# A gated linear-attention and recurrence kernel: one tile's normalisation shared with ScalarE, a subtraction in halves, and two orders on TensorE changed

## The reference, cut to what matters

```python
Q = elu(x @ Wq.T + bq) + 1;  K = elu(x @ Wk.T + bk) + 1;  V = x @ Wv.T + bv
KV = einsum('bnd,bne->bde', K, V)
Z  = einsum('bnd,bd->bn', Q, K.sum(axis=1) + 1e-06)
x1 = layernorm(x + (Q @ KV / Z) @ Wo.T + bo)
# recurrence over the first axis of x1
ft = sigmoid(xt @ wf.T + c @ uf.T + bf);  it = sigmoid(xt @ wi.T + c @ ui.T + bi)
gt = tanh(xt @ wc.T + c @ uc.T + bc);     c = ft * c + it * gt
h  = tanh(x1 @ wo.T + c_final @ uo.T + bo)
out = layernorm(x1 + h)
```

## Time and profile before

| | us |
|---|---|
| median of 3 runs (lowest, highest) | 101.58 (101.49, 101.75) |
| the profiled execution, its own time | 101.5 |
| its span in the profile | 99.4 |
| busy: TensorE matmuls | 89.9 |
| busy: VectorE | 80.0 |
| busy: ScalarE | 66.9 |
| busy: POOL (GpSimd) | 42.5 |

### The profile page before, as it was taken

One profiled execution on the slowest core, in us unless ns is written; L12 is line 12 of the kernel. 1 busy time (PEld: TensorE's weight loads), 2 busy tenths in 40 slices (PEclk: granted clock), 3 DMA queues, 4 the chain that ended last, 5 costly groups with the idle time before them and its releaser, 6 DMA issues.

```text
span 99.4 us, 1919 instructions
## 1 busy us (share of the span) xinstructions
PE 89.9 (90%) x607; PEld 78.3 (79%) x607; DVE 80.0 (81%) x227; ACT 66.9 (67%) x139; POOL 42.5 (43%) x71
## 2 busy tenths in 40 slices
PE   5998999999999999999999999999999999979100
PEld 4868879689588968978899899999999999957000
DVE  3254499979999996899589989999767897999660
ACT  1445779479597694885869445769495787897360
POOL 3006398327258058009405802440200435788850
PEclk9999999999999999999999999999999999999995
DMA  2868999100000000000000000000000003205336
GB/s 38 306 232 300 394 399 364 48 0 3 0 0 0 0 0 0 10 0 0 0 0 0 0 0 7 3 3 0 7 0 0 0 0 106 89 24 187 129 106 211
DMA packets 5413, 7.36 MB, mean 74 GB/s; under 512 B 507, under 2 KB 3228, under 8 KB 5404
## 3 DMA queue, kind: packets, MB, share of 16 engines
q1 hardware_dynamic: 4972, 6.92, 19.8%
q10 hardware_dynamic: 432, 0.33, 1.3%
HBM read 5.15 MB, written 2.10 MB: 73 GB/s over the span
## 4 chain that ended last, share of the span: by engine, by line
PE 75%; POOL 9%; DVE 4%; ACT 4%; issue 4%; DVEq 0%; POOLq 0%; ACTq 0%
PE ps_k L436 7%; PE ps_ctx L459 7%; PE ps_ctx L479 6%; PE ps_q L450 6%; POOL rstd L356 6%; PE ps_x L493 4%; PE ps_f L423 4%; PE ps_f L513 2%; PE ps_ctx L469 2%; PE ps_ctx L470 2%; PE ps_f L522 2%; PE ps_c L513 1%; PE ps_c L515 1%; PE ps_f L515 1%; PE ps_i L513 1%
## 5 line engine op out<-in xcount | busy, mean ns | idle before, releaser
L375 POOL TENSOR_TENSOR s_lo<-s,s_hi 128x512 fp32r<-128x512 f32 (+1 forms) x6 | 6.7, 1110 | 24.3 <-ACT s_hi L797 24.3
L331 POOL TENSOR_TENSOR rstd<-var_eps,minus_half 128x4 f32<-128x4 f32 x8 | 8.7, 1091 | 7.8 <-DVE var_eps L996 7.8
L322 POOL TENSOR_TENSOR k_pair<-k_rows 128x256 f32<-128x256 f32 x8 | 6.3, 783 | 8.9 <-DVE k_rows L1032 8.9
L1005 DVE TENSOR_SCALAR x<-x,stats,rstd 128x128 f32<-128x128 f32 x28 | 9.8, 408 | 0.0
L846 ACT ACTIVATE x_hi<-ps_x 128x512 fp32r<-128x512 f32 x8 | 4.8, 602 | 6.4 <-PE ps_x L493 6.4
L356 POOL TENSOR_TENSOR rstd<-var_eps,minus_half 128x4 f32<-128x4 f32 (+1 forms) x9 | 8.7, 965 | 0.5
L436 PE MATMUL ps_k<-wkq,x_cols 128*128 128x128 f32 x64 | 8.7, 279 | 0.0
L767 ACT ACTIVATE k_exp<-ps_k,minus_one 128x512 f32<-128x512 f32 x8 | 5.5, 686 | 4.6 <-PE ps_k L444 3.7
L436 PEld LDWEIGHTS ps_k<-wkq,x_cols 128*128 128x128 f32 x64 | 8.2, 197 | 0.3
L450 PE MATMUL ps_q<-x_cols,wkq 128*128 128x512 f32 x16 | 8.2, 593 | 0.0
L1020 DVE SCALAR_TENSOR_TENSOR x<-ps_ctx,z_inv,x_rows 128x128 f32<-128x128 f32 x28 | 8.0, 343 | 0.1
(11 more groups left out here) (211 smaller groups left out, 284.6 us busy)
## 6 DMA issues: line engine op xcount, KB each, us to landing
x_cols<-xt SPq DMA_DIRECT2D x8, 256.0 KB, 7.3
x_rows<-x SPq DMA_DIRECT2D x8, 256.0 KB, 7.3
out<-x SPq DMA_DIRECT2D x7, 256.0 KB, 2.2
wgate<-w_gate SPq DMA_DIRECT2D x1, 384.0 KB, 6.3
out<-x SPq DMA_DIRECT2D x2, 128.0 KB, 2.0
wkq<-w_kq ACTq DMA_DIRECT2D x1, 131.0 KB, 3.4
wvo_in<-w_vo_in ACTq DMA_DIRECT2D x1, 128.0 KB, 3.3
wout<-w_out SPq DMA_DIRECT2D x1, 128.0 KB, 7.0
```

Of the source, the lines that this page charges most:

```text
L322: nc.gpsimd.tensor_tensor(k_pair[:], k_rows[:, a % 2, 0:C // 2], k_rows[:, a % 2, C // 2:C], ALU.add).then_inc(k_pair_ok, 1)
L331: nc.gpsimd.tensor_tensor(rstd[:, b], var_eps[:, b], minus_half[:], ALU.pow).then_inc(rstd_ok, 1)
L375: nc.gpsimd.tensor_tensor(s_lo[:, t % 2, part], state(t)[:, part], s_hi[:, t % 2, part].bitcast(F32), ALU.subtract).then_inc(slo_ok[k], 1)
L1005: nc.vector.tensor_scalar(x1[:, b, c], x1[:, b, c], mean_of(b, c), rstd[:, b, c:c + 1], ALU.subtract, ALU.mult).then_inc(x1_ok, 1)
```

## The change

Four edits. (1) Tile 1 joins `SHARED_LN`, and in the period of step 0 ScalarE runs `forget_tanh(0)`, `first_normalise(1)`, `input_tanh(0)`, `key_bias(4)` in this order. (2) POOL makes the state's low part of step 3 in two halves, each counted; a step of the first half of the columns waits for one, a step of the second half for both. (3) Tile 7's `key_values` goes ahead of tile 6's `context` on TensorE, and ahead of `reciprocal_z(6)` on VectorE. (4) In the gates of entry 6 gates f and i get all three passes before gate c gets any.

```diff
--- before.py
+++ after.py
@@ -56,7 +56,7 24.00:53.00 29.00, 29.00 (x175) 23.95 (x175) 26.17 (x68) 21.58 (x38) 11.84 (x15) 1.00 0.00 1
 IN_PSUM = (6, 7, 8)
 
 
-SHARED_LN = (0, 6)
+SHARED_LN = (0, 1, 6)
 
 
 BIAS_BY_PE = 4
@@ -371,9 +371,11 24.00:53.00 29.00, 29.00 (x175) 23.95 (x175) 26.17 (x68) 21.58 (x38) 11.84 (x15) 1.00 0.00 1
 
             def state_low(k):
                 pool.wait_ge(shi_ok[k], 1)
-                t, part = STEPS[k][0], columns(k)
-                nc.gpsimd.tensor_tensor(s_lo[:, t % 2, part], state(t)[:, part], s_hi[:, t % 2, part].bitcast(F32),
-                                        ALU.subtract).then_inc(slo_ok[k], 1)
+                t, c0, c1 = STEPS[k]
+                for first, end in ((0, H), (H, C)) if k == 3 else ((c0, c1),):
+                    part = slice(first * D, end * D)
+                    nc.gpsimd.tensor_tensor(s_lo[:, t % 2, part], state(t)[:, part], s_hi[:, t % 2, part].bitcast(F32),
+                                            ALU.subtract).then_inc(slo_ok[k], 1)
 
             def halve_weights():
 
@@ -541,7 +543,7 24.00:53.00 29.00, 29.00 (x175) 23.95 (x175) 26.17 (x68) 21.58 (x38) 11.84 (x15) 1.00 0.00 1
                                  skip_group_check=True)
                 nc.tensor.matmul(ps[:, part], wgate_lo[:, u], s_hi[:, last, part], start=False, stop=False,
                                  skip_group_check=True)
-                pe.wait_ge(slo_ok[step_before(k)], 1)
+                pe.wait_ge(slo_ok[step_before(k)], 2 if step_before(k) == 3 and second_half(k) else 1)
                 nc.tensor.matmul(ps[:, part], wgate_hi[:, u], s_lo[:, last, part], start=False, stop=True,
                                  skip_group_check=True).then_inc(done, 1)
 
@@ -711,13 +713,18 24.00:53.00 29.00, 29.00 (x175) 23.95 (x175) 26.17 (x68) 21.58 (x38) 11.84 (x15) 1.00 0.00 1
             keys_x(7)
             gate_s(1, 4)
             gate_s(2, 4)
+            key_values(7)
             context(6)
-            key_values(7)
             x1_turned(5)
             context(7)
             gates_x(5)
             gates_s(5)
-            gates_x(6)
+            for g in (0, 1):
+                gate_x_high(g, 6)
+            for g in (0, 1):
+                gate_x_low(g, 6)
+            gate_x_high(2, 6)
+            gate_x_low(2, 6)
             gates_s(6)
             x1_turned(6)
             out_x(0)
@@ -881,7 +888,12 24.00:53.00 29.00, 29.00 (x175) 23.95 (x175) 26.17 (x68) 21.58 (x38) 11.84 (x15) 1.00 0.00 1
                     nc.scalar.activation(wgate_hi[:, 0:GATES], wgate[:, 0:GATES], ACT.Copy).then_inc(split_hi, 1)
                 if a > 2:
                     xk_copy(a)
-                if t is not None:
+                if t == 0:
+                    forget_tanh(t)
+                    first_normalise(b)
+                    input_tanh(t)
+                    key_bias(k + 1)
+                if t is not None and t >= 1:
                     forget_tanh(t)
                     key_bias(k + 1)
                     input_tanh(t)
```

## The result

| | before | after |
|---|---|---|
| median of 6 runs, us (lowest, highest) | 101.6 (101.41, 102.19) | 103.14 (102.56, 103.51) |
| ratio to before, 95% interval | | 1.0123 (1.0092 to 1.0153) |
| span of the profiled execution | 99.4 | 101.0 |

The account below looks back on a forecast made before the run. TensorE, busy 29.00 of 29 us from 24 to 53, was taken as the bound; +1.84 - 0.29 = +1.55, other edits 0, on 101.5 gave 103.05, stated as 103.1. Own range 102.9 to 103.4; with two rivals 102.5 to 103.7.

Parts of the forecast that it names:

- The copy behind the tanhs: Step 0's period: ScalarE's key_bias(4) runs after pair and both tanhs, so TensorE's keys(4) starts 1.84 us later.
- -0.29 for the transposes: Tile 1's transposes on TensorE no longer wait for VectorE's four normalising pieces: 0.29 us gained.
- rival 4: Copy wait at keys(4) isn't paid and all three TensorE waits fall away: 100.7 us; chance 0.04.
- The sum: Net effect in step 0's period, copy wait less transposes' gain: +1.84 - 0.29 = +1.55 us.
- 2.1 around it: Time outside the profiled execution's span of 99.4 us, counted as 2.1 us to make 101.5.
- The keys at 33.77: Profile row read as tile 6's, from which keys was taken as 0.89 us when nothing holds it.
- Halves, product, pass order at nothing: Edits 2 to 4, POOL's halves, tile 7's product first, entry 6's gate passes: each counted as 0 at the end.
- VectorE's `s` of step 4: VectorE's state operation, at 59.00 before: expected 1.55 us later although the wait in context(7) is gone.
- So VectorE, not TensorE, sets the time from 59 to 71.: VectorE runs nearly without a gap, busy 11.34 of 11.8 us, so TensorE's gains there count 0 to +0.03.
- The clock: TensorE's clock during the 1.84 us wait before keys(4): expected to stay at 1.00, nothing added.
- 1 (102.6): TensorE's gains at 57 to 63 us, -0.27 and -0.24, do count: 102.6 us; chance 0.12.
- 2 (103.6): More lateness: ScalarE doesn't overlap operations (+0.3) and POOL's k_sum(7) comes late (+0.15): 103.6 us; chance 0.10.

Follow-up runs that it names:

- copy last only: Kernel before, with only ScalarE's key_bias(4) moved behind input_tanh(0), VectorE keeping all four pieces of tile 1: 102.66 us, ratio 1.0092.
- copy first: Changed kernel with ScalarE's key_bias(4) put back right behind forget_tanh(0), ahead of tile 1's two pieces: 101.43 us, ratio 0.9972 to the kernel before.
- query_sum after: Kernel before, with VectorE's query_sum(3) run behind tile 1's four pieces instead of ahead of them: 102.18 us, ratio 1.0026.
- the last kernel of the table: Kernel before, with query_sum(3) behind tile 1's pieces and three instead of two of tile 6's pieces on ScalarE: 101.58 us, ratio 0.9972.

## Why the prediction was right, point by point

- **The copy behind the tanhs.** Right, and nearly to the digit: weights of `keys(4)` forecast at 25.84, found at 25.93 in an execution that runs 0.09 late. Pair at 23.20 (23.30), `th_i` 23.98 (24.08), `th_c` 24.55 (24.65), copy 25.12 (25.22). The step of 0.57 for a tanh and 0.78 for the pair held.
- **-0.29 for the transposes.** They did shrink to 0.44, and inside this change the 0.29 counts, as the 1.78 before it gave VectorE time to catch up (its idle 1.26). The sharing isn't what gave it: in copy last only, without sharing, they took 0.44 as well. But a gain of its own, as rival 4 took it for, it isn't: copy first and query_sum after each had it and ended within 0.02 of before. The weak step is "The transposes then have nothing to wait for: -0.29", read without asking what is late next. In the earlier trace rows VectorE stood at 26.17 of 29 us, and I drew on that only for what it could bear, not for what it was feeding.
- **The sum**, +1.55: 1.56 at `x1_low(5)`, 1.50 at the end. Right for the span. The runs' ratio gives 1.25 with an interval of 0.94 to 1.55, so the forecast is at its upper edge.
- **"2.1 around it"**, the step from span to time, taken as unchanged. Mis-sized: 1.79 with tile 1 shared, so by this term alone the time would be 0.3 below the forecast. That the median is 103.14 beside 103.1 is luck: the span of 99.4 that the sum starts from is a short one (the means of before in the three comparisons are 99.63 to 99.86), which makes up for it, and runs of the changed kernel lie 0.95 apart.
- **A misreading without effect.** The keys at 33.77 are tile 5's, not tile 6's.
- **Halves, product, pass order at nothing.** Nearly right: -0.01 alone, -0.11 on top of the first edit. POOL's halves took 1.42 together (I had 1.48), and nothing came late by them. VectorE's `s` of step 4 came 1.45 later and not 1.55 (60.54 against 59.00, less 0.09), and that 0.10 was gone again at `x1_low(5)`.
- **"So VectorE, not TensorE, sets the time from 59 to 71."** Half right. Right for what the change does and for added work (0.30 of 0.34), wrong as the only bound: with a piece off VectorE (0.26 by the expectation) it waits for TensorE's transposes.
- **The clock.** It didn't fall: granted 1.00 through 1.78 of idleness, `queries(4)` behind it at 0.86 as before. The Trainium skill's rule on long gaps (TensorE: Matmul & The Clock Gate, HAM oscillation) isn't touched by this; no run here has a longer gap ahead of work.
- **The rivals.** 1 (102.6) and 2 (103.6) lie near the result's spread, and the experiments decide against both: no gain of 0.5 at 57 to 63 us, and no further lateness. 4 would have needed the copy's end by 24.7; it was 25.81.

## What to carry to other kernels

When an instruction is given to an engine that has idle time, count not its own length but who waits for each instruction that it pushes back: here a pair of 0.78 on ScalarE cost 0.02 behind the copy that a saturated TensorE waits for, and 0.90 ahead of it. And a wait on the chain is only worth its length if its next feeder is early: look up when the producer of the following operand ends before counting it, as two lists that were tuned against each other are late together. A short operation moved to POOL beside VectorE's SBUF work can cost VectorE more than it saves (0.4 to 0.5 for 0.33 here).

## What the runs showed of the hardware that I hadn't expected

The executions of one kernel differ by up to 1.3 us (before: 101.23 to 102.56 in 35 executions). The profiles show where most of it arises: in the first matmuls behind the warm-up, above all in the eight of `keys(0)`. They take 1.22 in the kernel before, 1.14 after, and 1.91 in the last kernel of the table, with the same instructions, the granted clock at 1.00 in all three, and no wait shown:

```profile
4.61 1.22 PE L436 MATMUL ps_k<-wkq,x_cols 128*128 128x128 f32 x8
```

```profile
4.61 1.14 PE L438 MATMUL ps_k<-wkq,x_cols 128*128 128x128 f32 x8
```

```profile
4.61 1.91 PE L441 MATMUL ps_k<-wkq,x_cols 128*128 128x128 f32 x8
```

The same matmuls take 1.06 for `keys(1)`. In the last kernel the matmul behind the eight takes 0.77 as well, against 0.47 before. By `keys_x(0)` the three stand at 7.71, 7.81 and 8.61, and by `keys_x(2)` at 20.07, 20.16 and 20.98: the difference is made by then and stays. In all 14 profiled executions it is 12.35 to 12.37 from the one to the other, so a difference of 0.3 us inside the span is read more surely from the profile, counted from a common instruction, than from the times. How far the part behind `keys_x(2)` scatters from one execution of a kernel to the next isn't known, as each has one profile; hundredths there shouldn't be leaned on. And the profile doesn't see all: the 0.25 to 0.36 us that the kernels with tile 1 shared save outside the span shows only in time less span. What makes those first matmuls slow in some executions, and what that time outside is, stays open.
